# Output projection and layer norm of the cross attention, placed inside the attention stage

## The chip, the cores and the metric

One core of a Trainium2 chip. The time is device microseconds of one launch, median over runs.

## What is computed

Two perceiver layers, five residual blocks and a mixture of experts over 8 x 64 tokens of width 512. The change touches the fourth block, a cross attention from the 512 tokens to 8 contexts of 1601 rows (width 1024), 16 heads of 64, with one null key and value for each context. Its core:

```python
q = split_heads(x @ Wq); k, v = split_heads(context @ Wkv)      # layer-normed x
k, v = concat(null_k, k), concat(null_v, v)
attn = softmax(q @ k.T / 8)
out = (attn @ v).reshape(b, 64, 1024) @ Wout                      # projection, 1024 -> 512
out = (out - mean(out)) * rsqrt(var(out) + 1e-6) * ln_scale + ln_bias
x = x + out
```

The 512 tokens are four tiles of 128, two batches each.

## The kernel before

The cross attention has three stages. `queries` (L1654) makes q as two float16 parts, high and low, while the value products run (`ValueWork`, `QuadWork`), and copies them into `q_parts` in the buffer `work`: ACT the high part in two copies of 128x2048 (L1713), DVE the low part in two (L1731). QuadWork's load of the fourth raw buffer (L541) waits for the four copies.

`attend` (L1962) is a loop over steps t = 0 to 72, each engine with its program written out in that order. A step holds half a quad of key products (64 halves, so steps 0 to 63, `KeyWork`, banks `p_k`) and one pair of heads of one context: pair f = t - 8, 64 pairs, eight for each context. For a pair, PE computes 12 score matmuls into `p_s`, DVE the maximum (L2209), ACT the exponentials (L2163) and the high part of the weights (L2174), DVE the low part (L2227); SP transposes both parts by DMA (L2029, `turned`), PE multiplies with the values (L2129, L2132, 52 matmuls), which SP loads for each pair (L2017, L2019). POOL copies the pair's queries into a block diagonal (L2066). After four pairs DVE takes the result out of `p_o` into `o_t` (`leave`, L2236, L2238), in place of the queries in `work`. From pair 57 on (`TAIL`) there are no key products; then weights and values have second buffers in the room of the key work, and PE's values of pair f - 2 follow the scores of pair f. SP reloads x (1 MB, `x_kept`, L2047), which the key work had overwritten, in step 64, behind a DMA for the null value's row and a wait for it.

`project_out` (L2295) is a stage of its own behind `attend`: SP loads the weights (2 MB), scale and bias; DVE copies `o_t` into `heads`, tile by tile (L2334); PE projects the four tiles, 32 products of float32, 128x128 by 128x512 (L2321), each two passes in the trace; then DVE computes statistics (L2338, L2339), variance, reciprocal of ACT's root, and in four passes over each tile normalizes, scales, adds the bias and adds to x (L2346 to L2356). A stage ends with a barrier of all engines (`Stage.__exit__`). `head_attention` follows (its first DVE instruction is L2906).

Of the kernel before, what the change touches and what calls it, by code (L numbers as in the profile page):

```python
# [449 lines left out]
class QuadWork:  # L450
# [84 lines left out]
    def load(self, sp, k):  # L535
# [4 lines left out]
        elif k < self.RAWS:  # L540
            sp.wait_ge(self.moved, 2 * GROUPS)  # L541
        else:
            sp.wait_ge(self.op_lo, 3 * ((k - self.RAWS) // 2 + 1))
            sp.wait_ge(self.s_made, 4 * ((k - self.RAWS) // 2 + 1))
# [1109 lines left out]
def queries(nc, io, k, vw, x, xn, xt, q_parts, region, tk, first_raws, x_saved, ld_first):  # L1654

    with Stage(nc, "cq") as st:
# [47 lines left out]
        def _(act):  # L1705
# [6 lines left out]
            for g in range(GROUPS):  # L1712
                nc.scalar.activation(q_parts[:, :, g, 0, :, :],  # L1713
                                     q[:, 0, g * GP:(g + 1) * GP, :].rearrange("p c (b s) -> p b c s", b=B),
                                     ACT.Copy).then_inc(moved, 1)
            act.wait_ge(moved, 2 * GROUPS)
# [6 lines left out]
        def _(dve):  # L1723
# [6 lines left out]
            for g in range(GROUPS):  # L1730
                nc.vector.tensor_copy(q_parts[:, :, g, 1, :, :],  # L1731
                                      q[:, 1, g * GP:(g + 1) * GP, :].rearrange("p c (b s) -> p b c s", b=B))\
                    .then_inc(moved, 1)
# [228 lines left out]
def attend(nc, io, k, x, q_parts, o_t, vd, tk, rest, first_raws, ld_first, quads):  # L1962
    with Stage(nc, "ca") as st:
# [20 lines left out]
        ld_v = [st.sem(f"ld_v{s}") for s in range(2)]  # L1984
        block = st.block()
# [25 lines left out]
        def _(sp):  # L2011
# [25 lines left out]
            for t in range(STEPS):  # L2037
# [3 lines left out]
                if t == PARTS:  # L2041
                    sp.wait_ge(kw.op_lo, 3 * kw.QUADS)
                    sp.wait_ge(kw.s_lo, 4 * kw.QUADS)
                    sp.wait_ge(kw.prod, 7 * PARTS)
                    sp.dma_start(vals[1][LAST:LAST + 1, FULL, :, :], nv_parts).then_inc(null_set, 16)
                    sp.wait_ge(null_set, 32)
                    sp.dma_start(x[:, :, :], io.x_kept).then_inc(x_back, 16)  # L2047
                if f >= 1:
                    load_values(f)
                if f >= 0:  # L2050
# [7 lines left out]
        def _(g):  # L2058
            def diagonal(f):
# [5 lines left out]
                for h in range(2):  # L2065
                    g.tensor_copy(q_diag[f % 2][h * DH:(h + 1) * DH, :, h * S:(h + 1) * S],  # L2066
                                  q_parts[h * DH:(h + 1) * DH, b, p // GP, :, p % GP, :]).then_inc(q_ready, 1)
# [9 lines left out]
            for t in range(STEPS):  # L2077
# [15 lines left out]
        def _(pe):  # L2093
# [42 lines left out]

            for t in range(STEPS + 1):
# [65 lines left out]

        @block.vector
        def _(dve):
            def peak_of(f):
# [1375 lines left out]
```

## Time and profile before

| | |
|---|---|
| time, median of 3 runs | 3050.25 us (3048.16 to 3055.75) |
| profiled execution | 3043.98 us |
| its span | 3042.1 us |
| PE busy | 2772.9 us (91%), 21561 matmuls |
| DVE busy | 2013.8 us (66%) |
| ACT busy | 1188.6 us (39%) |
| POOL busy | 807.1 us (27%) |
| DMA | 343.88 MB, 113 GB/s in the mean |

The rows come from one profiled execution. Busy shares are means over stages with different limits, so what a change is worth is read from its stage. A timeline row is start (us from the span's start), duration, engine, line, operation, output<-input, count, and in brackets how long the engine stood before it and what it waited for. Granted clock 1.00 is 2.4 GHz, 0.50 is 1.2 GHz. `ca_` names belong to `attend`, `co_` to `project_out`, `ha_` to the heads' stage, `cq_` to the queries; `early_region` holds, in the tail, second buffers of weights and values.

### The profile page before, as it was taken

The page shows a single profiled execution, that of the slowest core. Times are in us where ns is not written, and L with a number is a line of the kernel's source. Part 1 is how long each engine was busy: PE and PEld are TensorE (multiplying, and loading weights), DVE is VectorE, ACT ScalarE, POOL GpSimd, SP SyncE. Part 2 cuts the span into 40 slices and gives each one's busy share as a digit, 9 for nine tenths or more (in the row PEclk, how much of TensorE's full clock was granted, in tenths as well). Part 3 has the DMA queues.
Part 4 walks back from the last instruction along what each step waited for, and adds up shares of the span by engine and source line. Part 5 has one row for each costly group of instructions (what it writes and reads, how often), then busy time and mean ns, then how long its engine had stood idle before and what let it go on. Part 6 is the DMA issues. An engine that isn't in the chain of part 4 may idle for free. (4 is left out here: it accounts for less than half of the span.)

```text
span 3042.1 us, 52549 instructions
## 1 busy us (share of the span) xinstructions
PE 2772.9 (91%) x21561; PEld 1824.6 (60%) x21569; DVE 2013.8 (66%) x2478; ACT 1188.6 (39%) x1853; POOL 807.1 (27%) x595
## 2 busy tenths in 40 slices
PE   6999999998989999979999999999999985786799
PEld 3334444443444444459999999999999973334453
DVE  5358999995564688855676777776667664467410
ACT  2254433431532444433444444444444433174210
POOL 1000000000000455545555455555455520100000
PEclk9999999999999999989999999999999997887899
DMA  5033334334423444421355555555555558100203
GB/s 205 24 107 105 97 101 135 97 95 153 134 83 104 134 136 133 125 79 67 100 133 133 133 133 141 138 141 139 143 141 133 133 128 187 60 7 22 111 24 128
DMA packets 471397, 343.88 MB, mean 113 GB/s; under 512 B 231955, under 2 KB 441172, under 8 KB 466678
## 3 DMA queue, kind: packets, MB, share of 16 engines
q1 hardware_dynamic: 471158, 340.52, 40.1%
q8 instruction: 171, 2.80, 0.4%
q14 instruction: 68, 0.56, 0.1%
HBM read 230.27 MB, written 55.67 MB: 94 GB/s over the span
## 5 line engine op out<-in xcount | busy, mean ns | idle before, releaser
L1905 PE MATMUL ca_p_k<-early_region,early_r 128*128 128x201 f16 (+1 forms) x2048 | 516.0, 252 | 35.1 <-DVE ca_held L1930 20.3
L1906 PE MATMUL ca_p_k<-early_region,early_r 128*128 128x201 f16 (+1 forms) x2048 | 511.9, 250 | 0.0
L1907 PE MATMUL ca_p_k<-early_region,early_r 128*128 128x201 f16 (+1 forms) x2048 | 511.7, 250 | 0.0
L1905 PE MATMUL ca_p_k<-early_region 128*128 128x201 f16 (+1 forms) x1536 | 385.0, 251 | 1.7 <-DVE ca_held L1930 1.6
L1906 PE MATMUL ca_p_k<-early_region 128*128 128x201 f16 (+1 forms) x1536 | 382.1, 249 | 0.0
L1907 PE MATMUL ca_p_k<-early_region 128*128 128x201 f16 (+1 forms) x1536 | 382.0, 249 | 0.0
L1930 DVE TENSOR_TENSOR ca_held<-ca_p_k,ca_held 128x402 f32<-128x402 f32 (+1 forms) x448 | 247.4, 568 | 142.6 <-PE ca_p_k L1907 141.8
L391 PE MATMUL vw_pv<-vw_wv,vw_ctx 128*128 128x512 f16 (+1 forms) x688 | 263.7, 383 | 35.7 <-PEq L74 15.1
L392 PE MATMUL vw_pv<-vw_wv,vw_ctx 128*128 128x512 f16 (+1 forms) x688 | 263.2, 383 | 0.0
L393 PE MATMUL vw_pv<-vw_wv,vw_ctx 128*128 128x512 f16 (+1 forms) x688 | 263.1, 382 | 0.0
L1948 ACT ACTIVATE ca_store<-ca_held 128x804 f16<-128x804 f32 (+2 forms) x128 | 111.8, 874 | 347.1 <-DVE ca_held L1930 342.5
L1952 DVE TENSOR_TENSOR ca_store<-ca_held,ca_store 128x804 f16<-128x804 f32 (+2 forms) x128 | 215.0, 1680 | 33.9 <-ACT ca_store L1948 33.9
L1905 PEld LDWEIGHTS ca_p_k<-early_region,early_r 128*128 128x128 f16 x2048 | 199.1, 97 | 46.5 <-DVE ca_held L1930 25.7
L605 POOL TENSOR_TENSOR cq_sums<-vw_ring 128x512 f32<-128x512 f32 x9 | 11.6, 1289 | 780.6 <-DMA vw_ring<-in_ctx_t 779.6
L1864 POOL TENSOR_TENSOR early_region<-x,early_region 128x804 f16<-128x804 f32 x64 | 152.8, 2387 | 212.5 <-ACT early_region L1873 212.5
L1906 PEld LDWEIGHTS ca_p_k<-early_region,early_r 128*128 128x128 f16 x2048 | 201.9, 99 | 2.4
L1907 PEld LDWEIGHTS ca_p_k<-early_region,early_r 128*128 128x128 f16 x2048 | 199.5, 97 | 0.4
L1307 ACT ACTIVATE work<-early_region,mb_a_neg 128x252 f32<-128x252 f32 x256 | 104.7, 492 | 219.1 <-DVE ms_h L1340 215.4
L2163 ACT ACTIVATE ca_probs<-ca_p_s,ca_small 128x1206 f32<-128x1206 f32 (+1 forms) x128 | 117.6, 924 | 170.7 <-DVE ca_small L2211 170.7
L2227 DVE SCALAR_TENSOR_TENSOR ca_parts<-ca_probs,ca_small,ca_parts 128x1602 f16<-128x1602 f32 x60 | 123.7, 2062 | 82.4 <-ACT ca_parts L2174 82.4
L1873 ACT ACTIVATE early_region<-x 128x804 f16<-128x804 f32 x128 | 110.6, 864 | 137.4 <-DMA x<-in_ctx_k 77.0
L1905 PEld LDWEIGHTS ca_p_k<-early_region 128*128 128x128 f16 x1536 | 148.5, 97 | 6.0 <-issue 2.1
(578 smaller groups left out, 6281.5 us busy)
## 6 DMA issues: line engine op xcount, KB each, us to landing
vd<-vw_vst SPq DMA_DIRECT2D x192, 256.0 KB, 2.3
ca_vals<-vd SPq DMA_DIRECT2D x60, 768.0 KB
vw_ring<-in_ctx_t SPq DMA_DIRECT2D x89, 512.0 KB, 4.0
x<-in_ctx_k SPq DMA_DIRECT2D x32, 804.0 KB, 4.5
early_region<-in_ctx_k SPq DMA_DIRECT2D x32, 804.0 KB, 6.9
ex_w_d<-in_w_d SPq DMA_DIRECT2D x8, 2048.0 KB, 7.9
vw_ring<-in_w_kv SPq DMA_DIRECT2D x16, 512.0 KB, 4.6
early_r<-state_rows SPq DMA_DIRECT2D x8, 1024.0 KB, 7.7
```

The source lines that it names most:

```text
L391: self.nc.tensor.matmul(o, xh[:, c, 0:w], self.wv[0][:, c, f], start=(c == 0), stop=False)
L392: self.nc.tensor.matmul(o, xh[:, c, 0:w], self.wv[1][:, c, f], start=False, stop=False)
L393: last = self.nc.tensor.matmul(o, xl[:, c, 0:w], self.wv[0][:, c, f], start=False, stop=(c == CC - 1))
L1864: g.tensor_tensor(s[:, 1, :], x, s[:, 0, :], ALU.subtract).then_inc(self.s_lo, 1)
L1905: self.nc.tensor.matmul(o[:, e, :], w[:, 0, c, f], x[:, 0, k], start=(c == 0), stop=False)
L1906: self.nc.tensor.matmul(o[:, e, :], w[:, 0, c, f], x[:, 1, k], start=False, stop=False)
L1907: last = self.nc.tensor.matmul(o[:, e, :], w[:, 1, c, f], x[:, 0, k], start=False, stop=(c == self.HALF - 1))
L1930: self.nc.vector.tensor_tensor(self.part(out, h, w), self.bank(m), self.part(other, h, w), ALU.add)\
L1948: self.nc.scalar.activation(self.out_place(i, k, 0), self.result(i, k), ACT.Copy).then_inc(self.out_hi, 1)
L1952: self.nc.vector.tensor_tensor(self.out_place(i, k, 1), self.result(i, k), self.out_place(i, k, 0), ALU.subtract)\
L2163: nc.scalar.activation(probs[:, COLS_OF[h][2]].rearrange("p (a n) -> p a n", n=COLS_OF[h][1]), scores(h), ACT.Exp, bias=nbias, scale=1.0 / ...
L2227: nc.vector.scalar_tensor_tensor(o[:, 1, 0:KEYS], probs[:, :], rinv, o[:, 0, 0:KEYS], ALU.mult, ALU.subtract).then_inc(wl_done, 1)
```

## The change

The stage `project_out` goes, and with it the copies into `heads`. `work` is laid out by tiles of tokens (t c b s), so that a tile of `o_t` is PE's stationary operand as it stands; the queries' copies become eight and eight, one per pair of heads. The weights, scale, bias and temporaries lie in `r1`, whose key weights are no longer needed. SP loads x in step 62, and weights, scale and bias in step 63 between the values and the transposes of pair 55; the null row is copied without a wait behind it. PE projects tiles 0 to 2 in halves of four products in steps f = 57 to 62, between scores and values, into the three banks of the key products; the first half of tile 3 before the last pair's values, the second behind them, into a bank of `p_s`. DVE takes statistics of tiles 0 to 2 at the end of steps 59, 61 and 63, normalizes these three, takes the last group out, then does tile 3. POOL adds the bias to x in steps 57 to 60, and scale and subtraction are one pass, so two passes over each tile stay on DVE.

The diff, its core:

```diff
         elif k < self.RAWS:
-            sp.wait_ge(self.moved, 2 * GROUPS)
+            sp.wait_ge(self.moved, 2 * PAIRS)
         else:
...
             act.wait_ge(q_low, PAIRS)
-            for g in range(GROUPS):
-                nc.scalar.activation(q_parts[:, :, g, 0, :, :],
-                                     q[:, 0, g * GP:(g + 1) * GP, :].rearrange("p c (b s) -> p b c s", b=B),
+            for c in range(PAIRS):
+                nc.scalar.activation(q_parts[:, :, c, :, 0, :],
+                                     q[:, 0, c, :].rearrange("p (t b s) -> p t b s", t=NT, b=2),
                                      ACT.Copy).then_inc(moved, 1)
-            act.wait_ge(moved, 2 * GROUPS)
+            act.wait_ge(moved, 2 * PAIRS)
             vw.act(act, LAST_UNITS - 2)
...
             dve.wait_ge(q_low, PAIRS)
-            for g in range(GROUPS):
-                nc.vector.tensor_copy(q_parts[:, :, g, 1, :, :],
-                                      q[:, 1, g * GP:(g + 1) * GP, :].rearrange("p c (b s) -> p b c s", b=B))\
-                    .then_inc(moved, 1)
+            for c in range(PAIRS):
+                nc.vector.tensor_copy(q_parts[:, :, c, :, 1, :],
+                                      q[:, 1, c, :].rearrange("p (t b s) -> p t b s", t=NT, b=2)).then_inc(moved, 1)
             vw.dve(dve, LAST_UNITS - 2)
...
 
-def attend(nc, io, k, x, q_parts, o_t, vd, tk, rest, first_raws, ld_first, quads):
+def attend(nc, io, k, x, q_parts, o_t, vd, tk, r1, rest, first_raws, ld_first, quads):
     with Stage(nc, "ca") as st:
...
         ld_v = [st.sem(f"ld_v{s}") for s in range(2)]
+        ld_w, ld_b, x_up, out_ready, var_ready, root_ready, ln_step = \
+            st.sems("ld_w ld_b x_up out_ready var_ready root_ready ln_step")
+        carve = Carve(r1.bitcast(f16))
+        w_out, scale, bias, normed = [carve.take(n) for n in ([P, PAIRS, D], [P, D], [P, D], [P, NT, D])]
+        stats, mv, var, root = [carve.take(n) for n in ([P, NT, 6], [P, NT, 2], [P, NT], [P, NT])]
+        p_out = [p_k[:, t * BANK:(t + 1) * BANK] for t in range(NT - 1)] + [p_s[:, 0:BANK]]
         block = st.block()
...
                     kw.load(sp, i + 1)
-                if t == PARTS:
+                if t == PARTS - 2:
                     sp.wait_ge(kw.op_lo, 3 * kw.QUADS)
                     sp.wait_ge(kw.s_lo, 4 * kw.QUADS)
+                    sp.wait_ge(null_set, 16)
+                    sp.dma_start(x[:, :, :], io.x_kept).then_inc(x_back, 16)
+                if t == PARTS:
                     sp.wait_ge(kw.prod, 7 * PARTS)
-                    sp.dma_start(vals[1][LAST:LAST + 1, FULL, :, :], nv_parts).then_inc(null_set, 16)
-                    sp.wait_ge(null_set, 32)
-                    sp.dma_start(x[:, :, :], io.x_kept).then_inc(x_back, 16)
+                    sp.dma_start(vals[1][LAST:LAST + 1, FULL, :, :], vals[0][LAST:LAST + 1, FULL, :, :]).then_inc(null_set, 16)
                 if f >= 1:
                     load_values(f)
+                if t == PARTS - 1:
+                    sp.wait_ge(kw.prod, 7 * (PARTS - 2) + 6)
+                    sp.dma_start(w_out, io.w_out).then_inc(ld_w, 16)
+                    sp.dma_start(scale, io.ln_scale.partition_broadcast(P)).then_inc(ld_b, 16)
+                    sp.dma_start(bias, io.ln_bias.partition_broadcast(P)).then_inc(ld_b, 16)
                 if f >= 0:
...
                     g.tensor_copy(q_diag[f % 2][h * DH:(h + 1) * DH, :, h * S:(h + 1) * S],
-                                  q_parts[h * DH:(h + 1) * DH, b, p // GP, :, p % GP, :]).then_inc(q_ready, 1)
+                                  q_parts[h * DH:(h + 1) * DH, b // 2, p, b % 2, :, :]).then_inc(q_ready, 1)
 
...
                     g.wait_ge(pad_zero, 2)
+                if f >= TAIL and f - TAIL < NT:
+                    g.wait_ge(x_back, 16)
+                    g.wait_ge(ld_b, 32)
+                    g.tensor_tensor(x[:, f - TAIL, :], x[:, f - TAIL, :], bias, ALU.add).then_inc(x_up, 1)
+                    g.wait_ge(x_up, f - TAIL + 1)
                 if t < PARTS and not later:
...
 
+            def project(t, first, n):
+                for c in range(first, first + n):
+                    last = nc.tensor.matmul(p_out[t], o_t[:, t, c, :, :].rearrange("p b s -> p (b s)"), w_out[:, c, :],
+                                            start=(c == 0), stop=(c == PAIRS - 1))
+                if first + n == PAIRS:
+                    last.then_inc(out_ready, 1)
+
             for t in range(STEPS + 1):
...
                     kw.pe(pe, 7 * t + 4)
+                if f == TAIL:
+                    pe.wait_ge(ld_w, 16)
+                    pe.wait_ge(kw.added, 14 * kw.QUADS)
+                    pe.wait_ge(o_copied, GROUPS * 2 * (NT - 1))
+                if TAIL <= f < TAIL + 2 * (NT - 1):
+                    project((f - TAIL) // 2, (f - TAIL) % 2 * GP, GP)
                 if 1 <= f < TAIL:
...
                     kw.pe(pe, 7 * t + 6)
+            pe.wait_ge(exp_done, 2 * NF)
+            pe.wait_ge(o_copied, NF // GP - 1)
+            project(NT - 1, 0, GP)
             attend_to(NF - 1)
+            pe.wait_ge(o_copied, NF // GP)
+            project(NT - 1, GP, GP)
 
...
 
+            for n, t in enumerate((slice(0, NT - 1), slice(NT - 1, NT))):
+                act.wait_ge(var_ready, n + 1)
+                nc.scalar.activation(root[:, t], var[:, t], ACT.Sqrt).then_inc(root_ready, 1)
+
         @block.vector
         def _(dve):
+            def statistics(t):
+                dve.wait_ge(out_ready, t + 1)
+                ln.link(nc.vector.bn_stats(stats[:, t, :], p_out[t]))
+                ln.link(nc.vector.bn_aggr(mv[:, t, :], stats[:, t, :]))
+
+            def normalize(n, first, last):
+                t = slice(first, last)
+                nc.vector.tensor_scalar(var[:, t], mv[:, t, 1], 1e-6, None, ALU.add).then_inc(var_ready, 1)
+                dve.wait_ge(root_ready, n + 1)
+                ln.link(nc.vector.reciprocal(var[:, t], root[:, t]))
+                for i in range(first, last):
+                    ln.mark(nc.vector.scalar_tensor_tensor(normed[:, i, :], p_out[i], mv[:, i, 0:1], scale,
+                                                           ALU.subtract, ALU.mult))
+                ln.settle()
+                for i in range(first, last):
+                    ln.mark(nc.vector.scalar_tensor_tensor(x[:, i, :], normed[:, i, :], var[:, i:i + 1], x[:, i, :],
+                                                           ALU.mult, ALU.add))
+                ln.settle()
+
+            ln = Chain(dve, ln_step)
+
             def peak_of(f):
...
                 both = p_o[:, :].rearrange("p (c l s) -> p l c s", l=2, s=S)
-                o = o_t[:, b, g * GP:(g + 1) * GP, :]
+                o = o_t[:, b // 2, g * GP:(g + 1) * GP, b % 2, :]
                 nc.vector.tensor_scalar(o, both[:, 0, :, :], 1.0 / (W_UP * P_UP), None, ALU.mult).then_inc(o_first, 1)
...
                     leave((f - 2) // GP)
+                if f >= TAIL + 2 and (f - TAIL) % 2 == 0:
+                    statistics((f - TAIL) // 2 - 1)
+            dve.wait_ge(x_up, NT)
+            dve.wait_ge(ld_b, 32)
+            normalize(0, 0, NT - 1)
             leave(NF // GP - 1)
-
-
-def project_out(nc, io, k, x, o_t):
...
+            statistics(NT - 1)
+            normalize(1, NT - 1, NT)
 
...
                 g.wait_ge(made, 5)
-        q_parts = work[:, :].bitcast(f16).rearrange("p (b g l c s) -> p b g l c s", b=B, g=GROUPS, l=2, c=GP)
-        o_t = work[:, :].rearrange("p (b c s) -> p b c s", b=B, c=PAIRS)
+        q_parts = work[:, :].bitcast(f16).rearrange("p (t c b l s) -> p t c b l s", t=NT, c=PAIRS, b=2, l=2)
+        o_t = work[:, :].rearrange("p (t c b s) -> p t c b s", t=NT, c=PAIRS, b=2)
         with Stage(nc, "early") as early:
...
                 queries(nc, io, k, vw, x, xn, xt, q_parts, region, tk, first_raws, x_saved, ld_first)
-            attend(nc, io, k, x, q_parts, o_t, io.vd, tk, region[:, 24 * 512:], first_raws, ld_first, vw.quads)
-        project_out(nc, io, k, x, o_t)
+            attend(nc, io, k, x, q_parts, o_t, io.vd, tk, r1, region[:, 24 * 512:], first_raws, ld_first, vw.quads)
         head_attention(nc, io, k, x, xn, xt)
```

## Rows read from the trace of the kernel before

**Rows 1.** The page: the granted TensorE clock in 40 slices, in tenths.

```profile
PEclk9999999999999999989999999999999997887899
```

**Rows 2.** Busy time by stretch: length, engines (instructions), clock, DMA share, GB/s.

```profile
2580.00:2590.00 10.00, 9.65 (x17) 4.28 (x18) 0.01 (x1) 0.00 (x0) 0.00 (x0) 0.73 0.09 32
2590.00:2600.00 10.00, 10.00 (x24) 4.37 (x23) 1.75 (x4) 0.00 (x0) 0.00 (x0) 1.00 0.00 0
2900.00:3042.00 142.00, 131.47 (x377) 63.67 (x375) 14.77 (x23) 13.52 (x27) 0.00 (x0) 0.97 0.21 82
```

**Rows 3.** Groups by line, 2571 to 2623.2: count | busy us, mean ns | idle before.

```profile
L2321 PE MATMUL co_p_out<-co_w,co_heads 128*128 128x512 f32 x64 | 30.2, 636 | 10.0 <-DMA co_w<-in_w_out 10.0
...
L2346 DVE TENSOR_SCALAR co_o<-co_p_out,co_mv,co_var 128x512 f32<-128x512 f32 x4 | 3.0, 806 | 0.0
L2338 DVE BATCH_NORM_STATS2 co_stats<-co_p_out 128x6 f32<-128x512 f32 x4 | 2.8, 698 | 32.7 <-PE co_p_out L2321 32.7
...
L2356 DVE TENSOR_TENSOR x<-x,co_o 128x512 f32<-128x512 f32 x4 | 2.5, 686 | 0.0
```

**Rows 4.** Timeline of DVE at the end of the removed stage: start, duration, [idle before].

```profile
2611.54 0.17 DVE L2341 TENSOR_SCALAR co_var<-co_mv 128x4 f32<-128x4 f32 x1
2611.99 0.18 DVE L2343 RECIPROCAL co_var<-co_root 128x4 f32<-128x4 f32 x1 [0.27 <-ACT co_root L2328]
...
2624.09 2.47 DVE L2906 BATCH_NORM_STATS2 ha_stats<-x 128x6 f32<-128x512 f32 x4 [1.33 <-PEq L74]
```

**Rows 5.** Timeline of ACT, 2560 to 2640: the table load at the stage's start.

```profile
2572.60 1.28 ACT L2328 ACT_TABLE_LOAD   x1 [10.57 <-PEq L74]
```

**Rows 6.** Timeline of DVE: tail: reductions of pairs 57 and 59, a low part.

```profile
2505.86 1.88 DVE L2209 TENSOR_REDUCE ca_small<-ca_p_s 128x1 f32<-128x1206 f32 x2
...
2520.42 1.89 DVE L2227 SCALAR_TENSOR_TENSOR ca_parts<-ca_probs,ca_small,ca_parts 128x1602 f16<-128x1602 f32 x1 [1.84 <-ACT ca_parts L2174]
2522.23 1.88 DVE L2209 TENSOR_REDUCE ca_small<-ca_p_s 128x1 f32<-128x1206 f32 x2
```

**Rows 7.** Timeline of DVE: the last pair's low part and the last group's first copy.

```profile
2562.11 1.89 DVE L2227 SCALAR_TENSOR_TENSOR early_region<-ca_probs,ca_small,early_region 128x1602 f16<-128x1602 f32 x1 [1.84 <-ACT early_region L2174]
2570.40 0.42 DVE L2236 TENSOR_SCALAR work<-ca_p_o 128x256 f32<-128x256 f32 x1 [6.40 <-PE ca_p_o L2132]
```

**Rows 8.** Busy time by stretch: one pair's step; the wait for the last transposes.

```profile
2518.28:2526.46 8.18, 3.46 (x64) 2.27 (x65) 4.28 (x7) 3.56 (x5) 2.11 (x2) 0.84 1.00 192
2564.00:2568.00 4.00, 0.00 (x0) 0.00 (x0) 0.00 (x1) 0.00 (x0) 0.00 (x0) 0.50 0.95 178
```

**Rows 9.** Busy time by stretch: key work just over; PE stops; clock falls; clock rises.

```profile
2496.00:2497.00 1.00, 1.00 (x7) 0.57 (x6) 0.12 (x1) 0.00 (x0) 0.00 (x0) 1.00 0.60 110
2503.00:2504.00 1.00, 0.33 (x2) 0.00 (x0) 0.74 (x1) 0.17 (x1) 0.51 (x1) 1.00 1.13 342
2506.00:2507.00 1.00, 0.00 (x0) 0.00 (x0) 1.00 (x1) 0.00 (x0) 0.00 (x0) 0.93 1.10 202
2513.00:2514.00 1.00, 1.00 (x6) 0.33 (x6) 1.00 (x1) 0.00 (x0) 0.00 (x0) 0.66 0.61 123
```

**Rows 10.** Timeline of SP's DMA issues around the end of the key work.

```profile
2490.00 4.80 SPq L2029 DMA_TRANSPOSE ca_turned<-ca_parts  x2
...
2497.36 0.35 SPq L2047 DMA_DIRECT2D x<-x_kept  x1
```

**Rows 11.** DMAs of the removed stage: packets, MB, share; KB and us to landing.

```profile
q1 hardware_dynamic: 432, 2.62, 13.6%
...
co_w<-in_w_out SPq DMA_DIRECT2D x1, 2048.0 KB, 7.7
```

**Rows 12.** Timeline of ACT and of PE where the queries are laid out.

```profile
1002.57 3.69 ACT L1713 ACTIVATE work<-early_region 128x2048 f16<-128x2048 f16 x2
...
1007.68 0.39 PE L391 MATMUL vw_pv<-vw_wv,vw_ctx 128*128 128x512 f16 x1 [0.71 <-DVE vw_vst L411]
```

**Rows 13.** Groups by line: POOL, whole span.

```profile
L605 POOL TENSOR_TENSOR cq_sums<-vw_ring 128x512 f32<-128x512 f32 x9 | 11.6, 1289 | 780.6 <-DMA vw_ring<-in_ctx_t 779.6 <-POOL cq_parts L620 0.7 <-POOL vw_ctx L620 0.3
```

More of the change, by code:

```diff
@@ L2291, in _ @@
                     leave((f - 2) // GP)
-            leave(NF // GP - 1)
-def project_out(nc, io, k, x, o_t):
-    with Stage(nc, "co") as st:
-        w = st.sb("w", [P, PAIRS, D])
-        scale, bias = st.sb("scale", [P, D]), st.sb("bias", [P, D])
-        o = st.sb("o", [P, NT, D])
-        heads = st.sb("heads", [P, PAIRS, TOK])
-        stats, mv = st.sb("stats", [P, NT, 6]), st.sb("mv", [P, NT, 2])
-        var, root = st.sb("var", [P, NT]), st.sb("root", [P, NT])
-        p_out = st.ps("p_out", NT)
-        ld_w, ld_b, moved, out_ready, var_ready, root_ready, chain = st.sems(
-            "ld_w ld_b moved out_ready var_ready root_ready chain")
-        block = st.block()
-        @block.sync
-        def _(sp):
-            sp.dma_start(w[:, :, :], io.w_out).then_inc(ld_w, 16)
-            sp.dma_start(scale[:, :], io.ln_scale.partition_broadcast(P)).then_inc(ld_b, 16)
-            sp.dma_start(bias[:, :], io.ln_bias.partition_broadcast(P)).then_inc(ld_b, 16)
-        @block.tensor
-        def _(pe):
-            pe.wait_ge(ld_w, 16)
-            for t in range(NT):
-                pe.wait_ge(moved, t + 1)
-                for f in range(PAIRS):
-                    last = nc.tensor.matmul(p_out[:, t * BANK:(t + 1) * BANK], heads[:, f, t * P:(t + 1) * P],
-                                            w[:, f, :], start=(f == 0), stop=(f == PAIRS - 1))
-                last.then_inc(out_ready, 1)
-        @block.scalar
-        def _(act):
-            act.wait_ge(var_ready, 1)
-            nc.scalar.activation(root[:, :], var[:, :], ACT.Sqrt).then_inc(root_ready, 1)
-        @block.vector
-        def _(dve):
-            c = Chain(dve, chain)
-            for t in range(NT):
-                nc.vector.tensor_copy(heads[:, :, t * P:(t + 1) * P].rearrange("p c (b s) -> p b c s", b=2),
-                                      o_t[:, 2 * t:2 * t + 2, :, :]).then_inc(moved, 1)
-            for t in range(NT):
-                dve.wait_ge(out_ready, t + 1)
-                c.link(nc.vector.bn_stats(stats[:, t, :], p_out[:, t * BANK:(t + 1) * BANK]))
-                c.mark(nc.vector.bn_aggr(mv[:, t, :], stats[:, t, :]))
-            c.settle()
-            nc.vector.tensor_scalar(var[:, :], mv[:, :, 1], 1e-6, None, ALU.add).then_inc(var_ready, 1)
-            dve.wait_ge(root_ready, 1)
-            c.link(nc.vector.reciprocal(var[:, :], root[:, :]))
-            dve.wait_ge(ld_b, 32)
-            for t in range(NT):
-                c.mark(nc.vector.tensor_scalar(o[:, t, :], p_out[:, t * BANK:(t + 1) * BANK], mv[:, t, 0:1],
-                                               var[:, t:t + 1], ALU.subtract, ALU.mult))
-            c.settle()
-            for t in range(NT):
-                c.mark(nc.vector.tensor_tensor(o[:, t, :], o[:, t, :], scale[:, :], ALU.mult))
-            c.settle()
-            for t in range(NT):
-                c.mark(nc.vector.tensor_tensor(o[:, t, :], o[:, t, :], bias[:, :], ALU.add))
-            c.settle()
-            for t in range(NT):
-                c.mark(nc.vector.tensor_tensor(x[:, t, :], x[:, t, :], o[:, t, :], ALU.add))
-            c.settle()
```

## The prediction

> **What bounds the kernel now.** I read, in this order, the page, busy time by stretch, the groups of the removed stage, the timelines of the last attention pairs engine by engine, and SP's queue. The profiled execution took 3043.98 us and its span is 3042.1, so 1.9 us lie around the span. The page shows the granted clock near full until slice 34 of 40 (76 us each), in which the tail of attention and the projection lie [rows 1]. That stage has one thing at work at a time. PE first stands 10.0 us waiting for the 2 MB of output weights, then works 30.2 us on 64 passes (32 products of type f32, two passes each), and the DVE waits 32.7 us for it meanwhile [rows 3]. DVE then does the layer norm alone, until the next stage's first DVE instruction at 2624.09 [rows 4]. Nothing of attention is left by then: DVE's last two copies start at 2570.40 [rows 7].
>
> In the tail (pairs 57 to 63, no key products any more) a pair takes (2522.23 - 2505.86) / 2 = 8.19 us, and DVE and ACT hand it to each other without a gap: reduction 1.88, exponentials on ACT, high part (DVE waits 1.84 for it), low part 1.89 from 2520.42, and the next reduction starts at 2522.23, as soon as the low part ends [rows 6]. PE is busy 3.46 of 8.18 us in such a step, 12 score matmuls and 52 of values, while the DMA engines' busy share is 1.00 [rows 8]. So PE has 4.7 us free per pair, DVE's order is the bound, and the DMA is close behind it.
>
> **The stage that goes.** From the end of the last pair's low part, 2562.11 + 1.89 = 2564.0 [rows 7], to the next stage's first DVE instruction at 2624.09 [rows 4] are 60.1 us. What stands there after the change is added up anew:
> - DVE: statistics of tile 2 (0.70 and an aggregation; 0.93 with the gaps), variance to the end of the reciprocal 0.63 (2611.54 to 2611.99 + 0.18, ACT's root inside it) [rows 3, 4]. Then three subtract-and-scale passes from PSUM at 0.75 each after the first (group mean 806 ns, overlapping by some 0.06) and three passes like the 686 ns additions, 0.63 each: 4.2 us [rows 3]. Together 5.9 us. In this time the last transposes land, at 4.0: PE does nothing from 2564 to 2568 and the DMA share is 0.95 [rows 8]. The last values end at about 5.3 if the clock is full. So the copies of the last group wait for DVE, not for PE, which costs about 0.5 us.
> - The last group's two copies, 0.42 each and a gap: 0.95 [rows 7]. They end at 6.9.
> - PE: the second half of tile 3 is 8 passes. Between 2590 and 2600, at granted clock 1.00, 23.3 passes took 10.00 us [rows 2], 0.43 each. 8 make 3.45; at 10.4.
> - DVE: statistics 0.93, variance to reciprocal 0.63, one pass from PSUM 0.81, one addition 0.69 [rows 3, 4]: 3.1; at 13.5.
> - The exit of the stages. Before, one gap of 1.33 stands here and a second (attention's exit) before the removed stage [rows 4, 5]. One of them stays: 15.0 us.
>
> 60.1 - 15.0 = **45.1 us gained**. The table load for the root (1.28 us) ran at the stage's start, long before its root [rows 5]; it now runs on ACT while ACT has nothing left, so it costs nothing. If it did wait for the variance, it would cost 1.3 us less what DVE has spare, some 0.8.
>
> The bounds of this block: the second half of tile 3 may find the clock low. From 2580 to 2590 the granted clock was 0.73 and only 17 passes were done [rows 2]; 8 passes at half rate are 6.9 us, so 0 to 3.5 us more. I take 0, as PE stands only some 1.6 us before it, having just done half of tile 3 and the last values.
>
> **What moves under the tail.** Tiles 0 to 2 are six halves of 8 passes, 3.45 us each, one in each step 57 to 62, placed between score and values. 3.46 + 3.45 = 6.9 of 8.19 us [rows 2, 8]: it fits at full clock. At half clock a step would be 13 us and would not fit. The rows show what the clock does: PE stopped 0.33 us into 2503 to 2504, still at 1.00, and the clock fell between 2506 and 2507 (0.93 there); it rose within 2513 to 2514 (0.66), while PE scored the next pair [rows 9]. With the projection PE stands 1.3 us per step, less than there, so I take full clock from step 58 on. The Trainium skill (TensorE: Matmul & The Clock Gate, "Part 1: The HAM clock gate") says that the throttled state is the default and activity releases it; that would make the added work pay part of itself back, and here it agrees with the rows. The opposite reading, f32 passes that leave the clock low, speaks against the change; it would stretch each of six steps by up to 4.9 us. The 2590 to 2600 row, f32 passes alone at 1.00, speaks against that.
>
> Statistics of tiles 0 and 1 are put behind the low part at steps 59 and 61, straight on DVE's chain: 2 x 0.93 = **1.9 us lost** [rows 3]. Their cost is known well (0.88 to 0.95 each).
>
> POOL adds the bias to x, four times 1.29 us [rows 13], in steps 57 to 60. Behind it wait the next diagonal copies, which may run a whole step ahead; it has 6 us idle per step (busy 2.11) [rows 8]. Nothing, unless the bias lands late; then PE's next score would wait for it.
>
> **DMA, queue by queue.** All are SP's. x comes back two steps earlier (it left the queue at 2497.36, behind a wait for the null row [rows 10]); it goes into a stretch where only the transfers of one pair are under way, and the wait on the null row is gone. Weights, scale and bias (2.62 MB) used 13.6% of 52 us of all 16 engines, 7.1 us [rows 11]; where the DMA is full its share reads 1.10 [rows 9], so I count 6.4 us. They now stand in SP's queue just ahead of pair 55's transposes, issued at 2490.00 [rows 10]. Those had landed at about 2496.6 (share 0.60 in 2496 to 2497 [rows 9]); with 6.4 us ahead of them they land at 2503. PE waits for them with the values of pair 55 and only then does score 57, of which DVE needs three banks of four to begin. Values at half clock took from 2568 to 2570.4 [rows 7, 8], and PE will have stood long enough for that: 2505.3. Score and values together took 3.46 us at 0.84 [rows 8]; less some 1.3 for the values, three quarters of the score are 1.6 at full and 3.2 at half clock, and I take 2.4: 2507.7, where DVE wanted it at 2505.86 [rows 6]. Were it otherwise this term would be 0. No row of before shows a load ahead of a transpose that was waited for.
>
> Since the share is 1.00 in the tail, I also asked whether this backlog stays. It need not: x's 1 MB leaves the tail, the weights of pair f are used two steps on, and the two statistics give 1.9 us.
>
> **Queries.** 2 + 2 copies become 8 + 8 of a quarter's size. On ACT the two take 3.69 us [rows 12]; six more starts at about 0.15 each make 0.9. ACT's next copy is what PE waited for (0.71 us idle at 1007.68) [rows 12], so **0.9 us lost** (0 to 1.5). DVE's small copies wait for the same ACT instruction and cost nothing.
>
> **Sum.** 45.1 - 1.9 - 1.8 - 0.9 = 40.5 us. From the execution profiled: 3043.98 - 40.5 = 3003.5. That execution lies 6.3 us under the median of 3050.25; on the median the sum gives 3009.8, which I forecast.
>
> **Rivals.**
> 1. *The DMA backlog comes through.* For: share 1.00 in the tail [rows 8], and 6.4 us put ahead of a transpose. Against: x has left. Then the first term is 6.4 and the last transposes are late too by the same, not in addition: 4.6 us more, 3014.4. Chance 0.15.
> 2. *PE becomes late.* The clock falls in some steps, scores come after the low part, and the last half of tile 3 goes at half rate: 3.5, and in two or three steps 2 to 4 us each: 8 to 15 us more, about 3021. For: 1.3 us of slack only; against: the rows on the clock. Chance 0.1.
> 3. *It does not do what it says.* If the three tiles queue up behind the last values instead of under the pairs, 48 passes x 0.43 = 20.6 us come back: 3030. The order in PE's program is fixed and all that tile 0 needs is there by step 57, so 0.02.
> 4. *Slower.* The removed stage ends 30 us of continuous PE work; what follows might find another clock. In the last 142 us the granted clock is 0.97 and PE busy 131.5 us [rows 2]. PE's time there goes as its inverse: at 0.97 x 131.5 / (131.5 + 40.5 + 9.2) = 0.70 the loss eats the gain and 9.2 us more, 3059. Below 0.70 it decides. Nothing of the change reaches that stage, and its PE is busy throughout: 0.02.
>
> The forecast has 0.71. The range takes in the low side (no DMA term, no query term, a run as far below the median as the profiled one) and rivals 1 and most of 2: 3001 to 3024. 0.3% is 9.2 us, about what a measurement can tell from no change; faster by more needs 31 us of losses not to occur: 0.95, same 0.03, slower 0.02.
>
> **What would show it.** In the changed profile: project matmuls between the scores and values of pairs 57 to 62, 8 passes in 3.4 us; the step at 8.2 us, with 0.93 more where statistics stand; pair 55's values at about 2503; no stage between attention and the heads; from the last low part to the heads' first instruction 15 us; ACT's small copies at about 4.6 us together. Wrong if a step shows DVE waiting for a score, if the granted clock in the tail stays at half, or if the last transposes land more than 5 us after the last low part.

## The result: 3016.8 us, 1.2% faster, and the profile after

| | before | after |
|---|---|---|
| median | 3051.47 us (3048.16 to 3055.75) | 3016.78 us (3012.25 to 3017.98) |
| profiled execution | 3043.98 us | 3016.38 us |
| its span | 3042.1 us | 3014.7 us |

The ratio is 0.9878, with a 95% interval of 0.9863 to 0.9893. Two later comparisons of the same two kernels gave 0.9866 and 0.9864. The forecast was 3009.8 us, the range 3001 to 3024. The gain is 34.7 us here, 43.1 and 39.4 in the later comparisons; 40.5 were forecast.

Times below are from the trace of the changed kernel unless another is named. Up to the end of the key work all lies some 4 us later than in the profile of before: the null key's copy starts at 2498.70, there at 2494.7.

The granted clock in 40 slices, from the page of the profile, answers to [rows 1]. The slice in which attention ended and the projection began stood at 7 there and stands at 9 here; the six behind it read 887899 in both.

```profile
PEclk9999999999999999989999999999999999887899
```

DVE's timeline from the last pair's low part to the heads' stage, against [rows 4, 7]:

```profile
2570.32 1.89 DVE L2286 SCALAR_TENSOR_TENSOR early_region<-ca_probs,ca_small,early_region 128x1602 f16<-128x1602 f32 x1 [1.84 <-ACT early_region L2208]
2572.12 0.69 DVE L2246 BATCH_NORM_STATS2 early_r<-ca_p_k 128x6 f32<-128x512 f32 x1
...
2573.51 0.18 DVE L2253 RECIPROCAL early_r<-early_r 128x3 f32<-128x3 f32 x1 [0.27 <-ACT early_r L2240]
2573.72 2.07 DVE L2255 SCALAR_TENSOR_TENSOR early_r<-ca_p_k,early_r 128x512 f32<-128x512 f32 x3
2575.82 2.08 DVE L2259 SCALAR_TENSOR_TENSOR x<-early_r,x 128x512 f32<-128x512 f32 x3
2577.93 0.42 DVE L2295 TENSOR_SCALAR work<-ca_p_o 128x256 f32<-128x256 f32 x1
...
2582.61 0.70 DVE L2246 BATCH_NORM_STATS2 early_r<-ca_p_s 128x6 f32<-128x512 f32 x1 [3.79 <-PE ca_p_s L2155]
...
2587.34 2.47 DVE L2907 BATCH_NORM_STATS2 ha_stats<-x 128x6 f32<-128x512 f32 x4 [1.62 <-PEq L74]
```

From the low part's end (2572.21) to the heads are 15.1 us (before, 60.1), and the order is the one foreseen: three tiles normalized, the last group's copies without a wait for PE, half a tile of passes, its statistics.

Busy time by stretch, columns as in [rows 2], of step 58, and of step 59, in which tile 0's statistics stand; below it PE's timeline: a half tile under a pair, and tile 3's last half.

```profile
2520.34:2528.53 8.19, 6.89 (x73) 3.77 (x72) 4.29 (x8) 3.56 (x5) 3.37 (x4) 1.00 1.07 202
2528.53:2537.65 9.12, 7.83 (x75) 4.15 (x75) 5.15 (x9) 3.56 (x5) 3.87 (x5) 1.00 1.25 226
```

```profile
2518.43 3.60 PE L2155 MATMUL ca_p_k<-early_r,work 128*128 128x512 f32 x8
...
2578.87 3.70 PE L2155 MATMUL ca_p_s<-early_r,work 128*128 128x512 f32 x8 [1.25 <-DVE work L2297]
```

Against [rows 8] PE's busy time in a step went from 3.46 to 6.89 us and the granted clock from 0.84 to 1.00, and the step kept its 8.19.

Beside the statistics, the tail became longer in one place, its start, at pairs 56 and 57. DVE's timeline against [rows 6], then ACT's, PE's and SP's of the same moment:

```profile
2500.84 1.89 DVE L2268 TENSOR_REDUCE ca_small<-ca_p_s 128x1 f32<-128x1206 f32 x2 [1.88 <-PE ca_p_s L2124]
...
2509.02 1.89 DVE L2286 SCALAR_TENSOR_TENSOR ca_parts<-ca_probs,ca_small,ca_parts 128x1602 f16<-128x1602 f32 x1 [3.64 <-ACT ca_parts L2208]
...
2511.28 0.42 DVE L2297 SCALAR_TENSOR_TENSOR work<-ca_p_o,work 128x256 f32<-128x256 f32 x1
2512.14 1.89 DVE L2268 TENSOR_REDUCE ca_small<-ca_p_s 128x1 f32<-128x1206 f32 x2 [0.44 <-PE ca_p_s L2124]
```

```profile
2507.30 1.63 ACT L2208 ACTIVATE ca_parts<-ca_probs,ca_small 128x1602 f16<-128x1602 f32 x1 [2.37 <-DMA ca_turned<-ca_parts]
```

```profile
2507.41 0.32 PE L2145 MATMUL ca_p_o<-ca_turned,ca_vals 128*64 128x128 f16 x2 [6.11 <-DMA ca_turned<-ca_parts]
...
2509.64 0.52 PE L2122 MATMUL ca_p_s<-ca_store,early_region 128*128 128x402 f16 x1
```

```profile
2493.49 0.35 SPq L2058 DMA_DIRECT2D early_r<-in_w_out  x1
...
2494.89 10.36 SPq L2034 DMA_TRANSPOSE ca_turned<-ca_parts  x2
2505.29 0.59 SPq L2053 DMA_DIRECT2D early_region<-ca_vals  x1
```

The queries' copies, ACT and PE, against [rows 12]:

```profile
1006.57 4.25 ACT L1713 ACTIVATE work<-early_region 128x512 f16<-128x512 f16 x8
```

```profile
1012.23 0.39 PE L391 MATMUL vw_pv<-vw_wv,vw_ctx 128*128 128x512 f16 x1 [1.27 <-DVE vw_vst L411]
```

All profiles cut at the same instructions, in us. "Start" runs to a product of the value work some 25 us behind the queries' copies (the first of L717 from `vw_wv` and `vw_ctx` into the banks `cq_p_q`); "key copy" is DVE's copy of the null key, "red." a pair's reduction, "heads" the first DVE instruction of their stage, "experts" the first matmul of theirs. after_five and after_six are the changed kernel too, best_two is best again; the others are told below.

| profile | start | key copy to red. 56 | red. 56 to 57 | red. 57 to last low part's end | to heads | heads to experts | span |
|---|---|---|---|---|---|---|---|
| before | 1031.0 | 2.14 | 8.98 | 58.14 | 60.09 | 245.7 | 3042.1 |
| again_before | 1030.8 | 3.40 | 8.98 | 58.16 | 60.04 | 252.3 | 3052.1 |
| third_before | 1029.5 | 2.13 | 8.98 | 58.14 | 60.14 | 252.5 | 3047.4 |
| fourth_before | 1031.8 | 3.44 | 8.99 | 58.14 | 60.83 | 248.1 | 3048.6 |
| after | 1035.6 | 2.14 | 11.30 | 60.07 | 15.13 | 255.0 | 3014.7 |
| again_after | 1036.8 | 3.57 | 10.35 | 60.05 | 15.13 | 253.3 | 3013.7 |
| after_five | 1033.8 | 2.59 | 12.07 | 60.07 | 15.13 | 253.0 | 3012.9 |
| after_six | 1031.8 | 2.58 | 10.60 | 60.07 | 16.82 | 252.9 | 3010.5 |
| w_behind | 1031.8 | 3.61 | 8.98 | 60.07 | 15.13 | 256.5 | 3010.6 |
| tiles_behind | 1031.3 | 2.14 | 11.34 | 58.16 | 40.09 | 253.1 | 3031.5 |
| stats_wait | 1031.9 | 2.14 | 11.60 | 58.38 | 14.91 | 253.0 | 3007.3 |
| w_more | 1033.1 | 3.51 | 14.07 | 60.06 | 15.14 | 255.3 | 3015.2 |
| best | 1035.6 | 3.61 | 8.98 | 58.38 | 14.92 | 253.2 | 3009.3 |
| best_two | 1030.8 | 2.13 | 8.98 | 58.37 | 14.93 | 255.4 | 3006.5 |

### The profile page after: what moved, and what is told of

It reads as the page before. It is cut to its first block and busy times, and to the rows that moved or that the text cites. A ratio compares the mean times of both kernels' runs of the same rounds, so it can differ in the third digit from the quotient of the medians.

```text
span 3014.7 us, 52539 instructions
## 1 busy us (share of the span) xinstructions
PE 2780.7 (92%) x21561; PEld 1828.6 (61%) x21569; DVE 2007.8 (67%) x2474; ACT 1189.3 (39%) x1860; POOL 813.8 (27%) x599
## 3 DMA queue, kind: packets, MB, share of 16 engines
q1 hardware_dynamic: 471158, 340.52, 40.5%
## 5 line engine op out<-in xcount | busy, mean ns | idle before, releaser
L391 PE MATMUL vw_pv<-vw_wv,vw_ctx 128*128 128x512 f16 (+1 forms) x688 | 265.3, 386 | 35.5 <-PEq L74 15.1
```

What stands on the lines that cost most here:

```text
L391: self.nc.tensor.matmul(o, xh[:, c, 0:w], self.wv[0][:, c, f], start=(c == 0), stop=False)
```

## The experiments

**The same two kernels again.** The first pair of profiles shows 27.4 us of gain in the span, though 36.75 had been won by the heads' start: 9.4 were lost in the heads' stage, whose code is the same.

> The kernel before, once more, for its profile. In the first pair of profiles 36.8 us had been gained when the heads' stage began, but 27.4 at the end: the heads' stage, whose code is the same, took 9.3 us less before than after, and another 3.6 us had gone before instruction L1000, also in unchanged code. Theory A (spread of an execution): the profile of before was a quick one (3043.98 against a median of 3051); this one takes 246 to 256 us from the heads' first DVE instruction to the experts' first product, against 245.7 in the first profile, and at least 3 us more than that. Theory B (the change costs the heads' stage, by the clock that it finds): again 245.7, within 1 us.

> The kernel after, once more, for its profile. Theory A (spread): the heads' stage, 255.0 us in the first profile, differs from that by some us either way. Theory B (caused): 255 within 1 us, and 9 us over before. In both: from the last pair's low part to the heads' first instruction 15.2 us, and the start of pair 57's reduction 2.3 us later against the end of the key work than before.

Measured: 3054.14 and 3015.58 us. The spans differ by 38.4 us this time, and the heads' stage by 1.0. The attention part repeats to some tenths in all that the change touches. So most of the 9.4 us was the one profile of before, a quick one; whether all of it was, these two leave open.

**The loads behind the transposes.** Weights, scale and bias go behind pair 55's transposes in SP's queue.

```diff
-                if t == PARTS - 1:
-                    sp.wait_ge(kw.prod, 7 * (PARTS - 2) + 6)
-                    sp.dma_start(w_out, io.w_out).then_inc(ld_w, 16)
...
                 if f >= 0:
                     turn(f, 0)
                     turn(f, 1)
+                if t == PARTS - 1:
+                    sp.wait_ge(kw.prod, 7 * (PARTS - 2) + 6)
+                    sp.dma_start(w_out, io.w_out).then_inc(ld_w, 16)
...
```

> The loads of weights, scale and bias go behind the transposes of pair 55 in SP's queue instead of ahead of them. Theory (the transposes stood behind 2.6 MB): they land some 6.4 us earlier, before the scores of pair 56 end; ACT's high part of pair 56 waits for DVE only, pair 57 begins 2.3 us earlier, and the rest of the tail is as it was: 2.3 us less in all, 0.1%, to be seen in the trace rather than the time. Rival (the DMA is full in the tail, so what is not lost there is lost later): pair 57 begins earlier, but transposes or values of pairs 56 to 58 come late and a later pair loses the 2.3 us again.

Measured: 3014.05 us, ratio 0.9874 (0.9846 to 0.9902). SP's, ACT's and DVE's timelines of this kernel, the two transposes of pair 55 and the two parts of pair 56:

```profile
2488.87 4.91 SPq L2034 DMA_TRANSPOSE ca_turned<-ca_parts  x2
2493.83 1.00 SPq L2063 DMA_DIRECT2D early_r<-in_w_out  x1
```

```profile
2502.26 1.63 ACT L2208 ACTIVATE ca_parts<-ca_probs,ca_small 128x1602 f16<-128x1602 f32 x1 [0.56 <-DVE ca_small L2278]
```

```profile
2503.98 1.89 DVE L2286 SCALAR_TENSOR_TENSOR ca_parts<-ca_probs,ca_small,ca_parts 128x1602 f16<-128x1602 f32 x1 [1.84 <-ACT ca_parts L2208]
```

SP's issue of the two transposes takes 4.91 us instead of 10.36, ACT waits for DVE only (0.56 us) and no longer for them, and the step from pair 56 to 57 is back at 8.98. Nothing comes later for it: the rest of the tail and the end are as before the move (60.07 and 15.13). So the longer step is the loads' place in the queue, and it is a choice, not a price of the change. In the time 2 us are less than these few executions tell apart.

**The tiles behind.** All project calls stand behind the last values, all statistics behind the last group's copies.

```diff
-                if TAIL <= f < TAIL + 2 * (NT - 1):
-                    project((f - TAIL) // 2, (f - TAIL) % 2 * GP, GP)
...
             attend_to(NF - 1)
+            for i in range(NT - 1):
+                project(i, 0, PAIRS)
...
-            project(NT - 1, GP, GP)
+            project(NT - 1, 0, PAIRS)
```

> The same stage, but PE projects all four tiles behind the last values, and all statistics follow there; loads, layout and the bias stay where the change put them. It tells what the place beside the pairs is worth, apart from what goes with the stage (barrier, copies, load wait, passes). Theory: 48 + 8 passes of 0.43 us come to stand behind the last values, 24.1 us, less 1.9 us of statistics that leave DVE's chain and some 1.5 of cover that the first half of tile 3 did not use: 20 to 21 us slower than after, about 3037, 14 us faster than before. Rival (the clock falls without PE work in the tail, and the tail's steps become PE-bound): slower by more, 24 us or more.

Measured: 3033.68 us, ratio 0.9942 (0.9923 to 0.9961), 19.6 us over w_behind on the same chip. DVE's and PE's timelines at the end:

```profile
2572.37 0.42 DVE L2293 TENSOR_SCALAR work<-ca_p_o 128x256 f32<-128x256 f32 x1 [6.41 <-PE ca_p_o L2148]
```

```profile
2572.26 22.10 PE L2155 MATMUL ca_p_k<-early_r,work 128*128 128x512 f32 x48
2594.20 7.03 PE L2155 MATMUL ca_p_s<-early_r,work 128*128 128x512 f32 x16
```

The heads start 40.09 us after the last low part instead of 15.13, and the tail has lost its 1.9 us of statistics: 23.1 us net. 56 passes more than in the changed kernel stand behind the last values, the first half of tile 3 among them: 24.1 us at 0.43 each, against 24.96 by which the end grew. This is what the place under the pairs is worth, some 2 us more than the 20 to 21 that I had expected. In the time it shows less: from the null key to the heads this trace is 23.9 us longer than w_behind's, but its heads' stage is 3.4 us shorter in that execution. The rest of the gain over before, 18.0 us in the time, does not depend on it: 10.0 of it are, by the row, the wait for the weights [rows 3].

**The changed kernel again, and the statistics in DVE's wait for the exponentials.** DVE waits 2.00 us for ACT's sums between a pair's maximum and its reciprocal; the statistics are placed there.

> The kernel after, timed in five rounds on the chip that also times its improvement below. The sum of the prediction, mended by what the traces showed (2.3 for 1.8 at pair 57, 0.6 for 0.9 in the queries), is 40.3 us; the four runs gave 34.7 with an interval of some 33 to 42. Theory (nothing is missing, the spread is the execution's): 36 to 42 us under before. Rival (the heads' stage pays some us for the change, by clock and by the landing of its loads): 33 to 36.

```diff
                 if pair:
                     peak_of(f)
...
+                if TAIL + 2 <= f < NF and (f - TAIL) % 2 == 0:
+                    statistics((f - TAIL) // 2 - 1)
                 if pair:
                     inverse(f)
...
-                if f >= TAIL + 2 and (f - TAIL) % 2 == 0:
-                    statistics((f - TAIL) // 2 - 1)
```

> Statistics of tiles 0 to 2 stand between a pair's maximum and its inverse sum, where DVE waits 2.0 us for ACT's exponentials, and not behind the low part. Theory (they were on the chain that DVE and ACT hand each other): from pair 57's reduction to the end of the last low part 58.1 us in place of 60.0, and from there to the heads' first instruction 0.3 us less (the last values then end after DVE has normalized). In all 2.2 us less. Rival (a DVE read of the products' banks holds up ACT or PE there): the wait for the exponentials grows, and less than 1 us comes of it.

Measured: after_five 3012.88 us, ratio 0.9866 (0.9846 to 0.9885), 43.1 us under before and 1 us more than the upper end expected; stats_wait 3009.16, one execution. Its tail is 58.38 against 60.07, and the end 14.91. Of the 1.9 us that the statistics cost the tail 0.2 are left; DVE's timeline of the kernel "best", which has the same edit, shows the place:

```profile
2528.88 0.69 DVE L2246 BATCH_NORM_STATS2 early_r<-ca_p_k 128x6 f32<-128x512 f32 x1
...
2531.03 0.21 DVE L2275 TENSOR_SCALAR ca_small<-ca_small 128x1 f32<-128x1 f32 x1 [1.25 <-ACT ca_probs L2197]
```

So the cost was in the place, and PE's products of a tile are there in time for the new one.

**One more megabyte ahead.** A load of 1 MB stands first, which nothing reads but for PE's wait.

```diff
+                    sp.dma_start(normed, io.w_out[:, 0:NT, :]).then_inc(ld_w, 16)
                     sp.dma_start(w_out, io.w_out).then_inc(ld_w, 16)
...
-                    pe.wait_ge(ld_w, 16)
+                    pe.wait_ge(ld_w, 32)
```

> One megabyte more is loaded ahead of the weights, to a place that is written again later; nothing reads it. Price of the suspected cost: theory (the transposes of pair 55 wait for all that stands ahead of them in the queue): 2.4 us more by the rate of the first loads, so pair 56's to pair 57's reduction grows from 11.3 (10.3 where pair 56 itself was late) to 13.7 us (12.7), and no later pair pays again. Rival (the engines serve the requests side by side): under 1 us, or the loss is spread over the later pairs.

Measured: 3017.11 us, one execution. SP's and DVE's timelines of this kernel:

```profile
2491.96 13.72 SPq L2034 DMA_TRANSPOSE ca_turned<-ca_parts  x2
```

```profile
2509.09 1.89 DVE L2287 SCALAR_TENSOR_TENSOR ca_parts<-ca_probs,ca_small,ca_parts 128x1602 f16<-128x1602 f32 x1 [6.16 <-ACT ca_parts L2209]
```

The issue takes 3.36 us more than in the profile of after, DVE's wait 2.5 more, and the step from 56 to 57 is 14.07 against 10.35 to 12.07 in the four profiles of the changed kernel (mean 11.08): 3.0 us for the megabyte, 2.0 to 3.7, from this one profile. My estimate from [rows 9, 11] was 6.4 us for 2.62 MB, 2.4 for one. That a load ahead costs time once the slack is used up is so; whether it is dearer than 2.4 the spread leaves open.

**Both mends and four copies for the queries.** "best" joins w_behind and stats_wait, and copies the queries in four and four pieces, one per tile.

```diff
-            for c in range(PAIRS):
-                nc.scalar.activation(q_parts[:, :, c, :, 0, :],
-                                     q[:, 0, c, :].rearrange("p (t b s) -> p t b s", t=NT, b=2),
+            for t in range(NT):
+                nc.scalar.activation(q_parts[:, t, :, :, 0, :],
+                                     q[:, 0, :, t * P:(t + 1) * P].rearrange("p c (b s) -> p c b s", b=2),
```

> Three edits together: the loads behind the transposes of pair 55, the statistics in DVE's wait for the exponentials, and the queries laid out in four and four copies by tile of tokens (128x1024) instead of eight and eight. Theory: 2.3 + 2.2 + 0.3 = 4.8 us under after, in the trace from the key work's end to the heads' first instruction 4.5 less, in the time 0.15%. Rival (the DMA is full in the tail): the last transposes land later than 4.2 us after the last low part, and the gain is under 3 us.

> The kernel after, beside its improvement once more. Theory: 36 to 42 us under before; 88.6 to 90 us from the last null key to the heads' first instruction.

> The three edits together, once more. In the first run the trace had 85.9 us from the last null key to the heads' first instruction where after has 88.6 to 89.9, and the time was 1.6 us under after's. Theory: 85.5 to 86 us again, and 2 to 5 us under after in the time. Rival: the difference in time is gone, or turns round, since executions differ by more.

Measured, the changed kernel and this one side by side: 3012.88 and 3011.26 us (after_five, best), then 3011.51 and 3008.90 (after_six, best_two). best_two's ratio is 0.986 (0.9846 to 0.9875), after_six's 0.9864 (0.9848 to 0.988). From the null key's copy to the heads its profiles have 85.9 and 84.4 us, the changed kernel's 88.6 to 90.1. ACT's copies went from 4.25 to 3.88 us, PE's wait from 1.27 to 0.91. About 4 us are gone in the trace, near the 4.5 expected, and 1.6 and 2.6 in the medians, where 4.8 were expected the first time; the intervals overlap, so that it is faster than the changed kernel is likely and not shown by the times.

**Before, twice more.** For what the heads' stage costs in either kernel, of which after_six above has the other side.

> The kernel before, a third profile, for the part in unchanged code. From the heads' first DVE instruction to the experts' first product the two profiles of before took 245.7 and 252.3 us, eight profiles of kernels without the projection stage 253.1 to 256.5. Theory (spread alone): this one and the next lie anywhere from 245 to 257, one of them over 253. Rival (the heads' stage pays for the change): both under 253.

> The kernel before, a fourth profile: as for the third. From the last null key to the heads' first instruction 129.4 to 131 us in any case.

Measured: 3049.39 and 3050.62 us, with 252.5 and 248.1 us for the heads, both under 253, as the second of the two readings has it. Four profiles of before now have 245.7 to 252.5 (mean 249.7), the four of the changed kernel 252.9 to 255.0 (mean 253.6), and the six of its variants 253.0 to 256.5. All ten lie above all four, though by 0.3 us only where they come closest. By chance alone the four would be the lowest of fourteen once in 1001 cases, so that the unchanged stage behind the change pays something for it is likely. The difference of the means is 3.9 us, and most of it comes from two quick executions of before (245.7 and 248.1), a kind that none of the ten is; how much the change costs there in the long run, four against four can't settle. PE's first passes in the heads and the stretches around them show a part of how. Timelines of PE, before, third_before, after:

```profile
2635.02 7.13 PE L2566 MATMUL ha_ps<-work,ha_wreg 128*64 128x256 f32 x64 [2.18 <-DVE work L2931]
```

```profile
2634.55 8.81 PE L2566 MATMUL ha_ps<-work,ha_wreg 128*64 128x256 f32 x64 [3.30 <-DVE work L2931]
```

```profile
2598.97 9.29 PE L2567 MATMUL ha_ps<-work,ha_wreg 128*64 128x256 f32 x64 [3.29 <-DVE work L2932]
```

Busy time by stretch, before: the first 10 us of the heads, the next 10, the whole stage.

```profile
2624.09:2634.09 10.00, 3.65 (x16) 3.28 (x16) 7.04 (x21) 2.46 (x5) 2.68 (x10) 0.55 0.94 318
2634.09:2644.09 10.00, 9.07 (x76) 6.31 (x78) 7.13 (x47) 5.01 (x11) 0.44 (x1) 1.00 0.33 135
...
2624.09:2869.80 245.71, 184.72 (x921) 94.81 (x921) 156.85 (x306) 117.92 (x211) 17.42 (x29) 0.85 0.12 42
```

After, the same:

```profile
2587.34:2597.34 10.00, 3.65 (x16) 3.28 (x16) 5.96 (x20) 1.77 (x4) 2.92 (x13) 0.50 0.86 277
2597.34:2607.34 10.00, 8.37 (x58) 5.78 (x60) 6.01 (x33) 3.39 (x8) 0.00 (x0) 0.70 0.43 176
...
2587.34:2842.40 255.06, 193.88 (x921) 99.54 (x921) 156.54 (x306) 117.92 (x211) 17.79 (x32) 0.80 0.12 40
```

In the first 10 us both kernels are at 0.50 to 0.55. In the second 10 us the granted clock is 1.00, 0.83, 0.83 and 1.00 in the four profiles of before, and 0.62 to 0.70 in the ten others, and PE's 64 matmuls take 7.13 to 8.81 us in the four and 9.24 to 10.00 in the ten. Later in the stage the clock falls and rises where PE waits for DVE; between 60 and 70 us it is at 0.50 in all ten and in two of before, at 0.64 and 0.65 in before's two quick ones. What sets the moment at which the clock rises, and why the change moves it later, no run here tells: PE had stood 18.6 us ahead of the heads' transposes in all four profiles of before, and 9.5 in all ten others. tiles_behind is one of the ten (253.1 us for the heads), so by this one profile the heads don't pay for the tiles' place under the pairs; the stage that went, or the shorter pause, may be the reason, which is not shown.

## Why the prediction was right, and where not

The time lies in the range, 7.0 us above the forecast in the first comparison, 3.1 and 1.7 in the other two. Step by step:

- **The stage that goes:** 45.1 forecast, 60.09 - 15.13 = 44.96. The copies didn't wait for PE, the table load showed nowhere, and the exit took 1.62. The terms that I had listed add up to 13.5 + 1.33 = 14.8 us, not to the 15.0 that I wrote; the exit, 0.3 longer than the gap taken for it, made up for the slip. The bound that I had kept for the last half of tile 3 at a low clock came in one profile of four, after_six, where PE's timeline has this row in place of the 3.70 above, and the heads start 16.82 us after the low part:

```profile
2575.25 5.40 PE L2155 MATMUL ca_p_s<-early_r,work 128*128 128x512 f32 x8 [1.25 <-DVE work L2297]
```

- **Tiles 0 to 2 under the pairs:** held. No reduction from pair 58 on waits for a score; 6.89 of 8.19 us at clock 1.00, as rival 2 would not have it. Rival 1 fell too: the DMA share of 1.07 and more in the steps keeps neither DVE nor ACT waiting. Rival 3 is the kernel tiles_behind, and cost 23.1 us net against the 20.6 that I gave it; in that kernel the first half of tile 3 stands behind too.
- **Statistics:** 1.9 forecast, 60.07 - 58.14 = 1.93, and avoidable.
- **Pair 55's transposes:** the landing was right. Forecast at 2503, with the 4.0 us by which this execution is late 2507.0; PE's values start at 2507.41. The issue of the two transposes goes from 4.80 [rows 10] to 10.36 us and they land late, and w_behind confirms that the place in the queue is the cause. The path that I argued is the one that ended last in three of the four profiles of the changed kernel. PE takes the values from 2507.41 and the scores of pair 57 from 2509.64 on, without a gap, and the reduction at 2512.14 waited 0.44 us for them (1.03 and 1.17 in again_after and after_five); the forecast of 2507.7, 4.0 us later, is 2511.7. Close beside it runs a second path, for which I had not asked. The high part of pair 56 goes into the buffer out of which pair 55's transposes still read, so ACT stood 2.37 us for them, DVE's low part behind it 3.64 instead of 1.84, and DVE's copies end at 2511.70, 0.44 us before the reduction. In after_six the reduction follows these copies without a wait, so there this second path decides. A transfer has readers of its target and writers of its source, and I had asked only for the first.
- **Queries:** 0.9 forecast, 0.56 measured on ACT (4.25 - 3.69) and at PE's wait (1.27 - 0.71). A further start costs 0.09 us; for the 0.15 that I took no row stood.
- **POOL's additions:** nothing, as forecast. Its busy time in a step is 3.4 to 3.9 of 8.2 to 9.1.
- **What follows:** this step failed. Rival 4 asked whether the next work finds another clock, and answered it with the last 142 us [rows 2], which are the experts; there it holds (172.2 to 172.4 us in all profiles). The heads between attention and the experts were left out. They begin with PE near half clock (0.50 to 0.55) and have waits throughout, and between the four profiles and the four they lose 3.9 us in the mean. "Nothing of the change reaches that stage" was wrong for the clock.

The sum mended for the parts of the change is 44.96 - 1.93 - 2.1 - 0.56 = 40.4. In the four profiles against four, the stretch from the null key to the heads gained 130.2 - 89.4 = 40.8, the heads gave 3.9 back, and 2.3 more went in the code ahead. Of these, 2.9 were lost before the queries' first product (L1697), in code that is the same, 0.8 between there and the end of the column "start", with the queries' copies in it, and 1.4 were gained between there and the null key. That gives 34.6, the difference of the mean spans. The first product of the queries starts at 923.5 to 925.9 us in before and at 924.7 to 930.0 in the ten others; whether the difference is chance stays open. The medians of the three comparisons, with more executions, gave 34.7, 43.1 and 39.4. As the forecast had nothing for the heads or for the code ahead, it is in part luck that the last two lie so near its 40.5; for the stretch from the null key to the heads it is not: 45.1 - 1.9 - 1.8 = 41.4 forecast, 40.8 measured.

## What to carry to other kernels

Work of an engine that stands idle under another's chain cost nothing here while its busy time stayed under the step (6.89 of 8.19 us), and its clock even rose with it. But put a load that nobody needs yet behind the transfers that someone does, as a queue hands its delay to the transfers' readers and to the writers of their source alike. DVE's statistics cost the tail 1.9 us at the end of a step and 0.2 in a wait inside it that was long enough for them: the place in the step decided. And when a stage is taken out, read the granted clock in the first stretches of the stage behind it, not that of the stretch nearest the end.

## What the runs showed of the hardware

- SP's issue of a pair's two DMA transposes took 3.4 to 7.4 us wherever no weights stood just ahead of them (pairs 0 to 63 of the fourteen profiles, but those that follow), 9.9 to 11.1 with 2.62 MB issued just before (six profiles; 10.36 in after), and 13.72 with 3.62 MB (w_more). The issue itself stands, and with it what follows in SP's program: the next issue in after starts at 2505.29.
- The same stage, with the same instructions and the same DVE and ACT busy time, took 245.7 to 256.5 us. In before and after PE was busy 184.7 and 193.9 us of it, at mean clocks 0.85 and 0.80.
- The score of the first pair after the null key (in the table, from the key's copy to the reduction) took 2.1 us in some executions and 3.4 to 3.6 in others, in both kernels, and 2.6 in two of the changed one, behind the same 2.9 us of an idle PE.
